# A graph layer's sender sums: nodes in 20 groups of 313, not 22 of 286

## The reference

```python
in_agg = jax.ops.segment_sum(edge_feat, receivers, num_segments=N_NODES)
out_agg = jax.ops.segment_sum(edge_feat, senders, num_segments=N_NODES)
to_updater = jnp.concatenate([in_agg, out_agg, node_feat], axis=1)   # [6250, 192]
h = jax.nn.relu(to_updater @ W1 + b1)                                # 256 hidden
x = _layernorm(x + (h @ W2 + b2), axis=-1)
```

## Time and profile before

| what | us |
|---|---|
| median of three runs | 1481.49 (1477.98 to 1488.18) |
| profiled execution | 1473.92 |
| its span | 1472.1 |
| TensorE busy | 1190.2 (81%), 23123 products |
| VectorE busy | 1213.3 (82%) |
| ScalarE busy | 991.9 (67%) |
| GpSimd busy | 1104.0 (75%) |
| mean granted TensorE clock | 0.967 of full |

### The profile page before, as it was taken

How to read it: one execution, slowest core, us unless ns; L and a number is a source line. 1 busy time by engine, 2 the same in 40 slices (tenths; PEclk the granted TensorE clock), 3 DMA queues, 4 the chain that set the end, 5 groups by cost and what they waited for, 6 DMA issues and landing times.

```text
span 1472.1 us, 63779 instructions
## 1 busy us (share of the span) xinstructions
PE 1190.2 (81%) x23123; PEld 976.6 (66%) x23123; DVE 1213.3 (82%) x3787; ACT 991.9 (67%) x2259; POOL 1104.0 (75%) x663
## 2 busy tenths in 40 slices
PE   3667678877888888888888888898888889898896
PEld 2646477767777777777777766666666666666743
DVE  6665788888888988889888888888888888888776
ACT  6334588878888888888888865566556556565432
POOL 3878777867688888877888788877776787777533
PEclk9976899999999999999999989999999999999998
DMA  9332599989899999999999988888878888887641
GB/s 294 31 40 17 90 195 197 195 182 195 174 208 202 195 202 207 196 192 200 210 236 226 218 207 204 186 191 190 206 177 195 202 200 193 201 189 168 151 133 59
DMA packets 262841, 263.21 MB, mean 179 GB/s; under 512 B 106099, under 2 KB 223956, under 8 KB 262486
## 3 DMA queue, kind: packets, MB, share of 16 engines
q1 hardware_dynamic: 170152, 231.66, 54.4%
q0 software_dynamic: 92384, 28.77, 26.2%
q10 hardware_dynamic: 144, 0.52, 0.1%
HBM read 146.90 MB, written 113.96 MB: 177 GB/s over the span
## 4 chain that ended last, share of the span: by engine, by line
PE 67%; issue 12%; ACT 8%; DVE 7%; DMA 2%; ACTq 1%; SPq 1%; DVEq 0%; another core or an unknown queue 0%; POOL 0%
PE psum L1677 24%; PE psum L1701 23%; PE psum L1653 6%; ACT slots_out L864 3%; PE psum L1755 2%; PE psum L1660 2%; DVE to_node L1324 2%; PE psum L1888 1%; PE psum L1616 1%; DMA feat<-in_edge_attr 1%; PE psum L1753 1%; PE psum L1843 1%; ACT again_sign L882 1%; DVE same L1351 1%; ACT parts L843 1%
## 5 line engine op out<-in xcount | busy, mean ns | idle before, releaser
L769 POOL DMA_INDIRECT out_tables<-payload,target x628 | 1070.6, 1705 | 297.5 <-issue 166.1
L1677 PE MATMUL psum<-parts,to_slot 128*128 128x194 bf16 x4836 | 476.5, 250 | 123.1 <-ACT slots_out L864 80.7
L1677 PEld LDWEIGHTS psum<-parts,to_slot 128*128 128x128 bf16 x4836 | 404.7, 98 | 166.3 <-ACT slots_out L864 97.1
L864 ACT ACTIVATE slots_out<-psum 128x388 bf16<-128x388 f32 x936 | 386.2, 473 | 104.2 <-PE psum L1677 78.3
L1701 PE MATMUL psum<-to_node,slots_in 64*64 64x286 bf16 x10296 | 391.2, 285 | 60.7 <-issue 51.6
L1701 PEld LDWEIGHTS psum<-to_node,slots_in 64*64 64x64 bf16 x10296 | 306.6, 106 | 133.4 <-issue 119.9
L1285 DVE TENSOR_SCALAR to_slot<-iota_h,slot 128x528 bf16<-128x528 f16 (+1 forms) x936 | 302.5, 371 | 59.8 <-PE psum L1677 38.2
L1324 DVE TENSOR_SCALAR to_node<-iota_h,slot_rel 128x286 bf16<-128x286 f16 x858 | 247.4, 309 | 20.2 <-PE psum L1701 19.5
L939 ACT ACTIVATE to_node<-apart 128x286 bf16<-128x286 bf16 x286 | 118.0, 436 | 114.6 <-PE psum L1701 113.4
L1324 DVE TENSOR_SCALAR to_node<-iota_rows,slot_rel 128x286 bf16<-128x286 f16 x572 | 194.4, 340 | 0.0
L1239 DVE TENSOR_TENSOR rest<-feat,parts 128x512 f32<-128x512 f32 (+1 forms) x176 | 131.1, 745 | 24.1 <-ACT parts L843 15.5
(11 more groups left out here) (138 smaller groups left out, 909.3 us busy)
## 6 DMA issues: line engine op xcount, KB each, us to landing
slot_tiles<-slots_out SPq DMA_DIRECT2D x156, 388.0 KB
feat<-in_edge_attr SPq DMA_DIRECT2D x195, 256.0 KB
slots_in<-slot_tiles SPq DMA_DIRECT2D x168, 242.5 KB
slots_in<-slot_tiles SPq DMA_DIRECT2D x168, 230.4 KB
slot_tiles<-slots_out SPq DMA_DIRECT2D x78, 291.0 KB
out_tables<-payload,target POOLq DMA_INDIRECT x628
out_tables<-zeros POOLq DMA_DIRECT2D x4, 1600.0 KB
feat<-out_tables SPq DMA_DIRECT2D x48, 128.0 KB, 2.3
```

The costliest lines, as they stand in the source:

```text
L769: e.indirect_dma_start(out_tab, at, payload[b][:, t, :], None, element_offset=k * TABLE_ROWS * D, compute_op=ALU.add).then_inc(s_tab[k], 16)
L864: e.activation(slots_out[b][:, g:g + n, m, :], ps_share[r % BANKS][:, 0:n * SLOT_W].rearrange("p (g w) -> p g w", w=SLOT_W), ACT.Copy).the ...
L1677: last = e.matmul(ps_share[r % BANKS][:, o:o + SLOT_W], to_slot[m][:, COLUMN_FROM[k] + t * P:COLUMN_FROM[k] + (t + 1) * P], parts[b][:, SH ...
```

## The change

GROUP_NODES becomes 313, so there are 20 groups and a batch has 10 slot tiles. The planner then gives 1, 2, 2, 2, 1, 1, 2, 6, 6, 6 products, 29 a batch, in 5 rounds of 3, 4, 2, 8 and 12; a chunk has 10 rounds, all of two tiles. Since 10 is not a multiple of the four banks, a chunk's first bank now depends on its parity (`round_bank`). The runs that `to_slots` compares are 480, 512, 544, 544, 480 and 480 wide (before 528, 576, 624, 544, 576 and 528). The order on TensorE is rounds 0 and 1, payload, 2 to 4, windows, 5 and 6, spread, 7 to 9; the stores of a chunk take 4, 4 and 2 tiles. In the summing stage there are 10 pairs of groups and 1560 tiles; the one-hot tiles are built 318 wide (HOT, 3 rows of 106 for the odd ones), and the products have 313 columns. The last pair of groups now uses the other two banks, so the banks of the hidden layer change places.

```diff
--- before.py
+++ after.py
@@ -73,7 +73,7 @@
 SHARE = MINIS * MINI
 SHARE_FROM = COLS - SHARE
 SLOTS = P // 2
-GROUP_NODES = 286
+GROUP_NODES = 313
 SLOT_GROUPS = -(-N_NODES // GROUP_NODES)
 NODE_PAIRS = SLOT_GROUPS // 2
 PAIR_NODES = 2 * GROUP_NODES
@@ -98,8 +98,8 @@
 COLUMN_FROM = [sum(COLUMN_SLOTS[:k]) for k in range(MINI + 1)]
 WIDEST = max(USED)
 TILE_COLUMNS = [[(k, tiles.index(t)) for k, tiles in enumerate(COLUMN_TILES) if t in tiles] for t in range(NODE_PAIRS)]
-HOT = GROUP_NODES
-HOT_ROW = 26
+HOT_ROW = 106
+HOT = -(-GROUP_NODES // HOT_ROW) * HOT_ROW
 SUMS = 16
 SHARE_CHUNKS = N_CHUNKS - FIRST - SUMS
 SHARE_PAIRS = SHARE_CHUNKS // 2
@@ -137,7 +137,7 @@
 assert len(RANK_BANKS) == 4 and GROUPS_IN_BANK * BATCH_TILES <= 512 and MINI * BATCH_TILES <= 512 and BATCH_TILES <= P
 assert HOT <= WIDEST and HOT % HOT_ROW == 0 and max(HOMES) <= SLOTS and len(set(HOMES)) == 1
 assert FIRST == 2 * BATCHES_OF_RANKS and SHARE_CHUNKS % 2 == 0 and OH_BUFS % ROUND == 0 and TILES % 2 == 0
-assert NODE_PAIRS % 2 == 1 and SLOT_GROUPS * GROUP_NODES <= TABLE_ROWS
+assert NODE_PAIRS % 2 == 0 and SLOT_GROUPS * GROUP_NODES <= TABLE_ROWS
 assert SHARE_FROM == QUAD == OUT_TABLES and COLS % OUT_TABLES == 0
 CODE = 0x3000
 POW = 60
@@ -274,10 +274,12 @@
             to_node = sb_middle("to_node", [P, OH_BUFS, HOT], bf16)
             apart = sb_middle("apart", [P, APARTS, HOT], bf16)
             slot_rel = [sb_middle(f"slot_rel{r}", [P, PART_TILES]) for r in range(RING)]
-            halves_sum = [sb_middle(f"halves_sum{h}", [P, HOT]) for h in range(2)]
+            halves_sum = [sb_middle(f"halves_sum{h}", [P, GROUP_NODES]) for h in range(2)]
             xT_flat = sb_middle("xT", [P, NT // GT * (GT // 2) * P + P])
-            used = (OH_BUFS + APARTS) * HOT // 2 + RING * PART_TILES + 2 * HOT + NT // GT * (GT // 2) * P + P
-            sb_middle("end_sharing", [P, MINIS * COLUMN_FROM[MINI] // 2 + NODE_PAIRS * MINIS * SLOT_W - used])
+            used = (OH_BUFS + APARTS) * HOT // 2 + RING * PART_TILES + 2 * GROUP_NODES + NT // GT * (GT // 2) * P + P
+            room_left = MINIS * COLUMN_FROM[MINI] // 2 + NODE_PAIRS * MINIS * SLOT_W - used
+            if room_left > 0:
+                sb_middle("end_sharing", [P, room_left])
             slots_in = [sb_middle(f"slots_in{r}", [P, PART_TILES, SLOT_W], bf16) for r in range(RING)]
             xs = sb_middle("xs", [P, N_TILES, D])
 
@@ -301,10 +303,10 @@
         ps_share = bank[4:8]
         ps_y = bank[2:4]
         ps_back = [bank[2 + b][:, 2 * P:4 * P] for b in range(2)]
-        ps_hid = [bank[6 - 2 * b:8 - 2 * b] for b in range(2)]
+        ps_hid = [bank[4 + 2 * b:6 + 2 * b] for b in range(2)]
         ps_groups = [bank[4 + 2 * k:6 + 2 * k] for k in range(2)]
         ps_turned = ps_pay[:, 0:2 * P]
-        ps_fold = [bank[n][D:2 * D, 0:HOT] for n in (3, 2)]
+        ps_fold = [bank[n][D:2 * D, 0:GROUP_NODES] for n in (3, 2)]
 
         s_cst = sem("s_cst")
         s_row = [sem(f"s_row{n}") for n in range(2)]
@@ -503,7 +505,11 @@
         HEAD_ROUNDS = ROUNDS
         FIRST_ROUNDS = 2
         BANKS = len(ps_share)
-        assert CHUNK_ROUNDS % BANKS == 0
+        assert MINIS * CHUNK_ROUNDS % BANKS == 0
+
+        def round_bank(b, r):
+
+            return ps_share[(CHUNK_ROUNDS * b + r) % BANKS]
 
         def turned_at(u):
 
@@ -862,7 +868,7 @@
                     m, g = r // ROUNDS, 2 * (r % ROUNDS)
                     n = min(2, NODE_PAIRS - g)
                     e.activation(slots_out[b][:, g:g + n, m, :],
-                                 ps_share[r % BANKS][:, 0:n * SLOT_W].rearrange("p (g w) -> p g w", w=SLOT_W),
+                                 round_bank(b, r)[:, 0:n * SLOT_W].rearrange("p (g w) -> p g w", w=SLOT_W),
                                  ACT.Copy).then_inc(s_slot_ev, 1)
 
             def share_columns():
@@ -967,7 +973,7 @@
 
                 e.wait_ge(s_fold, 2 * g + 1)
                 for h in range(2):
-                    last = e.activation(halves_sum[h][:, :], ps_groups[g % 2][h][:, 0:HOT], ACT.Copy)
+                    last = e.activation(halves_sum[h][:, :], ps_groups[g % 2][h][:, 0:GROUP_NODES], ACT.Copy)
                 last.then_inc(s_flush, 1)
 
             def put_sums(g, h, c):
@@ -1674,7 +1680,7 @@
                     o = g % 2 * SLOT_W
                     columns = TILE_COLUMNS[g]
                     for k, t in columns:
-                        last = e.matmul(ps_share[r % BANKS][:, o:o + SLOT_W], to_slot[m][:, COLUMN_FROM[k] + t * P:COLUMN_FROM[k] + (t + 1) * P],
+                        last = e.matmul(round_bank(b, r)[:, o:o + SLOT_W], to_slot[m][:, COLUMN_FROM[k] + t * P:COLUMN_FROM[k] + (t + 1) * P],
                                         parts[b][:, SHARE_FROM + MINI * m + k, 1:], start=((k, t) == columns[0]),
                                         stop=((k, t) == columns[-1]))
                 last.then_inc(s_slot, 1)
@@ -1698,9 +1704,9 @@
                 halves = [slice(SLOTS * h, SLOTS * (h + 1)) for h in range(2)]
                 def product(j, k, h, cols):
                     p, rows = part_of(j), halves[h]
-                    return e.matmul(ps_groups[g % 2][h][cols, 0:HOT],
+                    return e.matmul(ps_groups[g % 2][h][cols, 0:GROUP_NODES],
                                     slots_in[p % RING][rows, j - PART_FROM[p], D * k:D * (k + 1)],
-                                    to_node[rows, node_buf(g, j), :], start=(j == 0 and k < 2), stop=(j >= TILES - 2 and k == 2))
+                                    to_node[rows, node_buf(g, j), 0:GROUP_NODES], start=(j == 0 and k < 2), stop=(j >= TILES - 2 and k == 2))
 
                 for j in both:
                     for k in range(2):
```

## The result

The changed kernel takes 1384.43 us (median of four runs, 1382.03 to 1394.54), the kernel before 1482.49 on the same chip (four runs, 1477.98 to 1488.18): a ratio of 0.938 [0.933, 0.944]. The forecast was 1410 with 1376 to 1450 around it. The profiled execution took 1384.58 us against 1473.92, its span 1382.8 against 1472.1: 89.3 us went, where the sum had 72.

What follows compares the result with a forecast made beforehand. Sharing was taken as bound by the TensorE-ScalarE chain at 8.90 us a chunk, GpSimd's floor 8.38 right under it. Sharing 39, summing 27 and ranks 6 sum to 72 us: 1481.5 - 72 = 1410 us, range 1376 to 1450.

Steps and rivals of the forecast that it cites:

- (a) to (c): Sharing stage: fewer products, fewer evictions and reordered rounds take 1.1 us off the chain, 8.90 to 7.8 us a chunk.
- the second wait: Sharing stage: TensorE's 0.95 us wait before a batch's last 12-product round; 0.6 us more of it would be hidden.
- the first wait: Sharing stage: TensorE's 0.82 us wait for the first bank after the payload; 0.34 us of it would be filled.
- GpSimd is next: Sharing stage: GpSimd's scatters stop the fall at 8.40 us a chunk, 0.50 less, times 78 chunks 39 us.
- (f): Sharing stage: GpSimd's scatters stay as many and as long, a floor of 8.38 us a chunk.
- The first rival: Experiments' rival, sharing stage: the changed kernel is still bound by the chain, 0.86 us shorter by itself; no chance given.
- rival (2): Scatters shorten with fewer VectorE compares, leaving the DMA's floor; 70 us off sharing, 116 in all, 1366 us; chance 0.06.
- (e): Sharing stage: stores fall to 970 KB a chunk from 1067, so DMA needs 8.0 us a chunk.
- Summing: Summing stage: 936 fewer products, their pace likely set by instruction issue; 27 us less, ends 5 and 40.
- Rival (3): Summing stage: odd tiles' compare in three rows shuts scatters out, 2.15 us each; +24 us, 1505; chance 0.07.
- Rival (4): Wider groups overflow the 16 shared slots, forcing a second pass, far over 1.5 times the time; chance 0.01.
- Rival (1): Relief not passed on: sharing target waits stay, summing gaps add to streaming; 29 us less in all, 1452; chance 0.14.

Runs made afterwards that it cites:

- e10: The kernel before with the fourth scatter of each sharing chunk left out; 1465.7 us, ratio 1.008.
- e9: The changed kernel with the fourth scatter of each sharing chunk left out; 1354.1 us, ratio 0.928.
- e7: The kernel before with most sum products cut to 200 of 286 columns, sharing stage unaltered; 1449.2 us, ratio 0.996.
- e3: The changed kernel with 12 slot rounds a chunk again, adding two evictions and making four narrow; 1374.0 us, ratio 0.942.
- e4: The changed kernel with two zero products added in each sharing batch, 62 products a chunk again; 1366.6 us, ratio 0.937.
- e11: The changed kernel with every slot compare cut to 128 columns; 1379.8 us, ratio 0.948.
- e6: The changed kernel with the three 480-wide slot compares of a batch read in 3 rows of 160, the slower form; 1380.6 us, ratio 0.948.
- e1: The changed kernel with the fourth scatter of each sharing chunk adding 16 rows instead of 128; 1389.4 us, ratio 0.953.
- e12: The changed kernel unaltered, run again on another chip beside other variants; 1370.3 us, ratio 0.941.
- e8: The changed kernel with most sum products cut to 200 of 313 columns, sharing stage unaltered; 1365.3 us, ratio 0.938.
- e5: The changed kernel with slot compares widened from 3040 to 3328 columns a batch; 1377.3 us, ratio 0.944.
- e2: The kernel before with the fourth scatter of each sharing chunk adding 16 rows instead of 128; 1457.5 us, no ratio.

## Why the prediction was right, step by step

**The bound before** was read rightly, as far as it says that GpSimd stood under it. e10 shows it: a quarter of the scatters away, and the time does not fall. That the rest is the chain through the banks is read from the waits, and no run took the chain apart.

**The chain after** was 7.8 by the sum of (a) to (c), and e9 measured 7.79. So close a match is partly luck: from 8.89 the way is 1.1 us, from the 8.68 of e7 it is 0.9, the prices of single parts do not come back in full in e3 and e4, and VectorE alone is busy 7.3 us of each 7.79 in e9 (518 of 550). How the parts share in it was not tested one by one. The timeline bears out the second wait (29 products in one run), the first wait hardly (0.73 us, from 0.82), but there a chunk has time to spare, as it waits for GpSimd.

**GpSimd is next**: right, by e3 and e4 (work put back is free), e9 and the targets' row. The waits on slots_out did not quite fall as said: 32.4 us in 550 are 39 in 660, and I had said under 30.

**The term that was mis-sized is the floor in (f), "scatters are as many and as long: still 8.38 us".** As many, but 1.69 us long, not 1.774: a floor of 8.0 us, and 69.1 us off the stage, not 39. The first rival, the chain still the bound, is out by e9. That scatters give way was rival (2), at 8.0 us and 70 for the stage, and its size came true; its reason, fewer columns for VectorE to compare, is not borne out: e11 cut the compares by far more and the mean stayed at 1.675. What the traces show in its place is that the gain sits in one scatter of four, the second, from 1.970 to 1.644 us, and that in e6 and e11, with the compares changed, the long scatter moves to another place. The mean ranged over the runs from 1.591 (e10, long waits for targets) over 1.68 to 1.744 and 1.750 (e1, e9, each with changed scatters). So the length goes with when in a chunk a scatter falls; why that lengthens it is not shown, and the cause stays open. Nor was the DMA's 8.0 us of (e) the stop, by e1.

**By its own signs** the prediction was wrong in two of three: it named "if scatters change length", and they went from 1.774 to 1.689, and "if the sharing period moves by another amount than the waits on slots_out do", and it moved by 0.86 us where these fell by 0.57. The products' 45 ns did not come.

**Summing**: -21.7 against -27. The two ends of a product's price were 42.1 ns (issue) and 45.2 (gaps add to streaming); it came to 43.7 on the chip of the result, 42.2 in e12. e7 and e8 say that issue makes most of it: 86 columns are worth 1.6 ns, 0.02 a column, where the bursts change by (31.0 - 24.4)/86 = 0.08 a column. With 43.7 instead of 42.2 the 9360 products give back 14 of the 39 us, which leaves 25; the rest is within the waits for targets, 1.4 us a chunk still. So the likely value of 27 was right in kind: part of the relief went to GpSimd, as said. The other part, a dearer product, is not shown: at 0.02 ns a column 27 more columns are worth 0.5 ns and not 1.5, and in e12 the same program had 42.2.

**Ranks**: -5.5 against -6; every row went by its 20/22.

**The end**, "the output inside the 75 us behind", was taken as unchanged without a look, and it cost 6.9 us. The sums were ready, so it is no wait for data. The wait is 3.88 to 4.87 us in every variant of the changed kernel with its number of products (e1, e3, e5, e6, e8, e9, e11, and 4.12 in e12), 0.84 or 0.85 in e2, e7 and e10, and 0.91 in e4, the one variant of the changed kernel to which products were added, two a batch and in another stage. The chain of e4 there:

```profile
1295.25 0.91 issue
...
1297.51 3.70 PE psum L1897 x8
```

The end of e4 behind the last sum product took 75.7 us, e12's 80.9. So instructions that cost nothing where they stand go with 5 us less of wait elsewhere, which is where e4's 1366.6 against 1370.3 may come from. The traces say more about this wait. It is one instruction of TensorE's sequencer, the branch that jumps over the second pass: it takes 4.16 us in the changed kernel, 0.50 in the kernel before and 0.57 in e4. Of the DMA queues that bring instructions, the view of 1304.8 to 1309.2 us has:

```profile
q8 instruction: 1, 0.02, 1.3%
q14 instruction: 1, 0.01, 0.9%
```

The q8 packet, 16 KB, begins 1.8 us after the branch. In all nine traces with the long wait such a packet begins 1.0 to 1.8 us into the branch, and the branch ends 1.5 us after the packet has come (1.47 to 1.51 us). In e4 it began 1.9 us ahead of the branch, which again ended 1.5 us after it; in the four traces of the kernel before it began 3.7 to 4.2 us ahead, and the branch took 0.50 us. (The q14 packet lies near the branch in all fourteen traces.) The Trainium skill (Runtime: NRT & Kernel Launch, "Instruction fetch mechanics") says that a taken branch to a page not at hand makes the engine wait for its fetch, and the traces agree. So the long wait is one for instructions. What is not shown is why they came in time in e4: that the added products shift the code behind them against the fetch is a guess, and no run moved the code alone.

**Rival (3)** is dead: the odd form in three rows kept its slower pace (351 against 325 ns) and the scatters beside it their 1.6 us. (Its limit for a loss, 2.02 us, leaves out the 6 us of the ranks; with them it is 2.05.) **Rival (4)** too: no second pass. **Rival (1)** would have left waits for targets, and 5.5 us of them are left. In the sum two errors of 30 and 5 us and one of 7 met, and that was luck: without the 5 and the 7 us the time would have been 1384 - 12 = 1372 us, under the range's 1376. The measured gain of the medians is 98 us, 9 more than that of the profiled executions, since the profiled one of before lay 4 us under the fastest of its four others.

## What to carry to other kernels

Where the engine next in line stands half a microsecond under the period, its own floor decides what a relief is worth; treat the length of its instructions as a quantity with a spread of its own (here 1.59 to 1.78 us in the mean of one and the same scatter) and carry that into the range. A mean over unlike instructions can move by one of them alone, so split it by place before looking for a cause. The length of the program can also decide where waits without data fall, so look at the stages that a change doesn't touch. To find out which of two near bounds holds, take a whole instruction out of one in both kernels: shortening it may not shorten anything. And a stream of small products with gaps of issue between its bursts is priced by the instruction rather than by the column, as long as its pace stays above that of the bursts.
